# Quantised feed-forwards that turn shifted floats on TensorE, and a GpSimd sum taken in halves

## The reference, cut to what matters

```python
# block 0: int8.  lhs is layernorm(x), rhs a 128x128 weight
lhs_scale = max(|lhs| over features, 1e-12) / 127
q_lhs = clip(round(lhs / lhs_scale), -127, 127)
out = (q_lhs @ q_rhs) * lhs_scale * rhs_scale
# block 1: ternary weight, 8 bit rows
z = clip(x / a_scale * 127, -128, 127);  y = round(z) @ w_quant.T * (w_scale * a_scale / 127)
# block 3, SwitchHead: 8 heads h, 8 experts e, two of them chosen per row and head
xv  = einsum('bsd,hedp->bshep', x, v_w);   v = einsum('bshep,bshe->bhsp', xv, gate_v)
ctx = softmax(q k / sqrt(P)) @ v
out = einsum('bshep,hepd->bsd', ctx[..., None, :] * gate_o[..., None], o_w)
```

## Time and profile before

| | us |
|---|---|
| median of 3 runs | 3508.23 |
| the profiled execution | 3510.38 |
| its span, from first to last instruction | 3508.5 |
| busy in the span: PE, DVE, ACT, POOL | 3139.7, 3014.5, 2281.8, 2265.1 |
| feed-forward of layer 0 | about 209 to 297 |
| feed-forward of layer 1 | about 641 to 717 |
| SwitchHead stage | about 1575 to 3508 |

### The profile page before, as it was taken

The page is one execution under the profiler, slowest core; times in us unless marked ns, Lnnn a source line. Parts: engine busy times, 40 slices in busy tenths (PEclk is TensorE's granted clock), DMA queues, the critical chain, the costliest instruction groups (busy, mean ns, idle before and its releaser), DMA issues.

```text
span 3508.5 us, 80049 instructions
## 1 busy us (share of the span) xinstructions
PE 3139.7 (89%) x24877; PEld 2286.1 (65%) x24890; DVE 3014.5 (86%) x9644; ACT 2281.8 (65%) x7501; POOL 2265.1 (65%) x2884
## 2 busy tenths in 40 slices
PE   6944999369986599949999999999999999999999
PEld 3522777246654377737777777777777777777777
DVE  4455999679989799958999999999999999999998
ACT  2355666721139666646777777777777777777777
POOL 1246999444448766615777777777777777777777
PEclk9999999555557699969999999999999999999999
DMA  1101000011100001140000000000000000000000
GB/s 53 56 4 19 16 16 14 1 45 45 45 21 1 10 29 31 30 121 6 8 8 8 8 7 8 8 8 7 7 8 8 8 8 8 8 8 8 8 7 6
DMA packets 135142, 63.82 MB, mean 18 GB/s; under 512 B 22592, under 2 KB 134336, under 8 KB 134720
## 3 DMA queue, kind: packets, MB, share of 16 engines
q1 hardware_dynamic: 134720, 58.70, 6.1%
HBM read 41.81 MB, written 8.45 MB: 14 GB/s over the span
## 4 chain that ended last, share of the span: by engine, by line
PE 43%; DVE 10%; issue 1%; POOL 0%; ACT 0%; DMA 0%; POOLq 0%; SPq 0%; DVEq 0%; ACTq 0%
PE ps_sw_d L1968 16%; PE ps_sw_a L1968 15%; DVE sw_o_part L1870 6%; PE ps_sw_w L2010 4%; PE ps_sw_w L1997 3%; PE ps_sw_s L1983 2%; PE ps_sw_s L2021 2%; DVE sw_gate_v L1900 1%; DVE sw_ctx_low L1916 1%; PE ps_sw_m L1988 1%; DVE sw_m_inv L1897 0%; PE ps_sw_m L1976 0%; DVE sw_mv L220 0%; DVE sw_v_part L1870 0%; DVE sw_norm L1898 0%
## 5 line engine op out<-in xcount | busy, mean ns | idle before, releaser
L1756 ACT ACTIVATE sw_scaled<-ps_sw_a,sw_gate_o 128x128 f32<-128x128 f32 x2048 | 620.5, 447 | 251.5 <-PE ps_sw_a L1968 243.4
L1756 ACT ACTIVATE sw_scaled<-ps_sw_a,sw_gate_v 128x128 f32<-128x128 f32 x2048 | 597.3, 445 | 217.3 <-PE ps_sw_a L1968 217.1
L1723 POOL TENSOR_TENSOR sw_o_rest<-sw_o_rest,sw_scaled 128x512 f32<-128x512 f32 x384 | 498.7, 1299 | 200.6 <-ACT sw_scaled L1756 199.2
L1870 DVE SCALAR_TENSOR_TENSOR sw_o_part<-ps_sw_d,sw_gate_o,sw_o_part 128x128 f32<-128x128 f32 x1920 | 555.5, 338 | 26.5 <-PE ps_sw_d L1968 25.3
L1703 POOL TENSOR_TENSOR sw_v_pair<-sw_v_part,sw_scaled 128x256 f32<-128x256 f32 x512 | 377.1, 737 | 248.3 <-DVE sw_v_part L1870 164.8
L1870 DVE SCALAR_TENSOR_TENSOR sw_v_part<-ps_sw_d,sw_gate_v,sw_scaled 128x128 f32<-128x128 f32 x1024 | 302.6, 335 | 90.1 <-PE ps_sw_d L1968 86.7
L1870 DVE SCALAR_TENSOR_TENSOR sw_v_part<-ps_sw_d,sw_gate_v,sw_v_part 128x128 f32<-128x128 f32 x1024 | 302.5, 334 | 0.0
L1708 POOL TENSOR_TENSOR sw_v<-sw_v_pair 128x128 f32<-128x128 f32 x512 | 235.8, 460 | 40.2
L920 POOL TENSOR_TENSOR at_key_wide<-at_keyT,c_half_heads 128x1024 f32<-128x1024 f32 x128 | 242.6, 1896 | 4.2 <-ACT at_keyT L1017 4.2
L1968 PE MATMUL ps_sw_a<-sw_v_high,sw_xT_high 128*128 128x512 f32 x512 | 225.9, 441 | 0.3 <-ACT sw_scaled L1756 0.3
L1968 PE MATMUL ps_sw_a<-sw_o_high,sw_ctx_high 128*128 128x512 f32 x512 | 214.6, 419 | 0.0
(11 more groups left out here) (314 smaller groups left out, 8897.6 us busy)
## 6 DMA issues: line engine op xcount, KB each, us to landing
at_ctxT<-ctx_T SPq DMA_DIRECT2D x128, 64.0 KB, 1.8
re_values<-in_ctx SPq DMA_DIRECT2D x128, 64.0 KB, 2.3
x<-in_x SPq DMA_DIRECT2D x64, 64.0 KB, 1.8
l_ctx<-in_ctx SPq DMA_DIRECT2D x64, 64.0 KB, 2.0
re_ctx<-in_ctx SPq DMA_DIRECT2D x64, 64.0 KB, 1.9
scratch_x<-x SPq DMA_DIRECT2D x64, 64.0 KB, 1.8
swp_staged<-in_L_ffn_v_w SPq DMA_DIRECT2D x8, 512.0 KB, 5.5
swp_staged<-in_L_ffn_o_w SPq DMA_DIRECT2D x8, 512.0 KB, 6.9
```

The costliest lines, as they stand in the source:

```text
L1723: pool.tensor_tensor(o_rest[:], o_rest[:], scaled[:, h % 4], ALU.add).then_inc(pooled["o"], 1)
L1756: act.activation(scaled[:, h % 4, e], ps_a[h % 2][:, e], ACT.Copy, scale=gates[:, s, h, HALF_E + e:HALF_E + e + 1]).then_inc(a_scaled[kind ...
L1870: dve.scalar_tensor_tensor(out=acc[:, e % 2], in0=ps_d[h % 2][:, e], scalar=gates[:, s, h, e:e + 1], in1=before, op0=ALU.mult, op1=ALU.add ...
```

## The change

Three edits.

1. In both quantised feed-forwards DVE's subtraction L716 and its buffer go. PE turns the shifted floats themselves, 32 bits wide, into a PSUM bank of floats. ACT's copy out of that bank adds -ROUND and writes bf16.
2. The lags behind it shrink by one: turning 4 to 3, copy and product 5 to 4, output and POOL's add 6 to 5. The shift's buffer is free when it has been turned, no longer when it has been rounded.
3. In the SwitchHead stage each of POOL's sums into `o_rest` becomes two of 128x256, the second behind a wait for the first.

```diff
-        q16 = k.sb(name + "_q16", [P, NB, N, P], BF16)
-        ps_q = [k.psum(f"{name}_q{n}", [P, N, P], BF16) for n in range(2)]
+        ps_q = [k.psum(f"{name}_q{n}", [P, N, P]) for n in range(2)]
...
-                in_order(([(0, spread)] if layer == 0 else []) + [(6, add), (1, rstd)], GROUPS)
+                in_order(([(0, spread)] if layer == 0 else []) + [(5, add), (1, rstd)], GROUPS)
...
-                def rounded(g, s):
-                    dve.wait_ge(q["shifted"], N * g + N)
-                    if g >= NB:
-                        dve.wait_ge(q["turned"], g - NB + 1)
-                    dve.tensor_scalar(q16[:, s], shifted[:, s], ROUND, None, ALU.subtract).then_inc(q["rounded"], 1)
...
-                steps += ([(3, output_scale)] if layer == 1 else []) + [(4, rounded), (1, variance)]
+                steps += ([(3, output_scale)] if layer == 1 else []) + [(1, variance)]
...
-                    act.activation(qT[:, s], ps_q[g % 2], ACT.Copy).then_inc(q["qT"], 1)
+                    act.activation(qT[:, s], ps_q[g % 2], ACT.Copy, bias=-ROUND).then_inc(q["qT"], 1)
...
-                        act.wait_ge(q["rounded"], g - NB + 1)
+                        act.wait_ge(q["turned"], g - NB + 1)
...
-                in_order([(6, output), (2, normalise), (5, keep), (3, shift)], GROUPS)
+                in_order([(5, output), (2, normalise), (4, keep), (3, shift)], GROUPS)
...
-                    pe.wait_ge(q["rounded"], g + 1)
+                    pe.wait_ge(q["shifted"], N * g + N)
...
-                        m = pe.transpose(ps_q[g % 2][:, n], q16[:, s, n], C["ident16"][:])
+                        m = pe.transpose(ps_q[g % 2][:, n], shifted[:, s, n], C["ident"][:])
...
-                in_order(([(0, turn_rows)] if layer == 0 else []) + [(5, product), (4, turned)], GROUPS)
+                in_order(([(0, turn_rows)] if layer == 0 else []) + [(4, product), (3, turned)], GROUPS)
...
-                            pool.tensor_tensor(o_rest[:], scaled[:, 0], scaled[:, 1], ALU.add).then_inc(pooled["o"], 2)
+                            pool.tensor_tensor(o_rest[:, 0:2], scaled[:, 0, 0:2], scaled[:, 1, 0:2], ALU.add)\
+                                .then_inc(q["o_half"], 2)
+                            pool.wait_ge(q["o_half"], u + 1)
+                            pool.tensor_tensor(o_rest[:, 2:4], scaled[:, 0, 2:4], scaled[:, 1, 2:4], ALU.add)\
+                                .then_inc(pooled["o"], 2)
...
-                            pool.tensor_tensor(o_rest[:], o_rest[:], scaled[:, h % 4], ALU.add).then_inc(pooled["o"], 1)
+                            pool.tensor_tensor(o_rest[:, 0:2], o_rest[:, 0:2], scaled[:, h % 4, 0:2], ALU.add)\
+                                .then_inc(q["o_half"], 1)
+                            pool.wait_ge(q["o_half"], u + 1)
+                            pool.tensor_tensor(o_rest[:, 2:4], o_rest[:, 2:4], scaled[:, h % 4, 2:4], ALU.add)\
+                                .then_inc(pooled["o"], 1)
```

More of the change, by code:

```diff
@@ L632, in feed_forward_int @@
         ps_rows = [k.psum(f"{name}_rows{n}", [P, N, P]) for n in range(2)] if layer == 0 else None
-        ps_q = [k.psum(f"{name}_q{n}", [P, N, P], BF16) for n in range(2)]
+        ps_q = [k.psum(f"{name}_q{n}", [P, N, P]) for n in range(2)]
         ps_y = [k.psum(f"{name}_y{n}", [P, N, P]) for n in range(2)]
         q = k.sems(name, "spread", "rows", "added", "stats", "moments", "var_eps", "rstd", "nmr", "xhat", "absmax", "scale",
-                   "inverse", "out_scale", "shifted", "rounded", "turned", "qT", "product", "y", "weighed", "x")
+                   "inverse", "out_scale", "shifted", "turned", "qT", "product", "y", "weighed", "x")
         y_scale = small["scale"] if layer == 0 else small["out_scale"]
@@ L1650, in switch_attention @@
                    "ranked", "u", "uT", "scores", "top", "shift", "exp", "p_turned", "p_kept", "rsum",
-                   "ctx", "ctx_high", "ctx_low", "v", "v_paired", "o_first", "o_added", "o_paired", "y")
+                   "ctx", "ctx_high", "ctx_low", "v", "v_paired", "o_first", "o_added", "o_paired", "o_half", "y")
         a_made = {n: k.sem("sw_a_made_" + n) for n in "vo"}
```

## The result

| | before | after |
|---|---|---|
| median of 22 runs each | 3507.18 | 3493.86 |
| the profiled execution's span | 3508.5 | 3495.5 |

What follows compares the result with a forecast made beforehand. It took a DVE-POOL loop to bound layer 0, ACT layer 1, PE with DVE waits the SwitchHead stage. -7.5 - 1.2 + 2.8 - 11.4 = -17.3 us, from 3508.2 to 3491; forecast's own range 3486 to 3499, whole range 3475 to 3515.

Steps and rivals of the forecast that it cites:

- part 1: Layer 0's feed-forward: removing L716 and shortening the lag saves 7.5 us, between 3 and 9.
- So POOL becomes the bound, at 4.28: Layer 0's feed-forward: without L716 the slot falls from 4.72 to POOL's 4.28 us, 0.44 saved in some 11 slots.
- The two terms ahead of the drain: Layer 0's feed-forward: -4.8 us from some 11 steady slots and -0.5 from earlier slots without large POOL work.
- The drain, -2.5: End of layer 0's feed-forward: the shorter lag leaves POOL three pairs instead of four, saving 2.5 us.
- part 3: SwitchHead stage: halving POOL's sums saves 11.4 us in the steady tiles and costs 2.8 at the end.
- Part 2: Layer 1's feed-forward: ACT stays full, so only start and drain gain; -1.2 us, between +1 and -2.5.
- Both DVE waits of PE go or nearly so: SwitchHead stage: L1900 ends 0.35 us earlier, so PE's bank d loads hardly wait for DVE's sums.
- ACT's hold on the a load: SwitchHead stage: ACT's sums for o unit 7 become what PE's bank a load waits for, allowing it at 2057.80.
- the 0.19: SwitchHead stage: us saved per tile once ACT is the next bound; over some 60 tiles -11.4 us.
- 12 x 0.23: End of the SwitchHead stage: 12 unhidden POOL sums, each 0.23 us longer when halved, cost 2.8 us.
- Rival (c): SwitchHead stage: L1900 meets the second half of POOL's sum and ends 0.4 us later; 3520 us, chance 0.19.
- Rival (d): Layer 1's feed-forward and retention: denser turns raise PE's clock from 0.50 to 1.00; 3477 us, chance 0.04.

Runs made afterwards that it cites:

- e17: Changed kernel with the feed-forwards' absolute maxima and moments in PSUM and whole POOL sums in the last tile; 0.9950 of the kernel before, 17.7 us less.
- e6: Changed kernel with the old, longer lags in the feed-forwards; layer 0 86.5 us against the changed kernel's 84.6, layer 1 75.5 against 74.4.
- e3: Changed kernel with whole instead of halved POOL sums in the last SwitchHead tile; 0.9960 of the kernel before, 14.0 us less.
- e8: Changed kernel with unread extra PE matmuls in layer 1's feed-forward to keep PE busy; 0.9958 of the kernel before.

## Why the prediction was wrong

Two steps failed: one in the sum of part 1, worth 4 us, and one that the sum doesn't have at all, worth 20.

**The step that failed in part 1 is "So POOL becomes the bound, at 4.28".** DVE's removed 0.49 us did leave the loop of DVE and POOL, but the slot fell by 0.17, not 0.44. I compared three bounds and left out a fourth, the loop of the rows above, which was 4.55 us long all the time. I missed it because I took DVE's durations as fixed. The scale was 0.47 long, of which 0.15 is its own; the rest was waiting for POOL's L651. Whenever the scale starts, it ends with POOL's multiplication, 1.29 us after that began before the change and 1.30 after it: it started 0.82 us behind and took 0.47, now it starts 0.66 behind and takes 0.64. The two terms ahead of the drain were forecast at -4.8 and -0.5 and are -1.5 together. e17 took the lock away and kept the order, and the slot was 4.25: the 4.28 was POOL's right bound, the lock the missing term. The low end of the range, "the three near-equal bounds trip over each other at 4.5", had the size, without the mechanism. The drain, -2.5, measured -1.95 (e6 1.85).

**The total against the measured ratio.** -17.3 us was forecast, 0.9951 or 3491. The ratio of 0.9905 makes it 3475, far below the forecast's own range of 3486 to 3499. The step that failed here is that the sum holds the three touched stages only and puts all others at nothing: the first stage took 47 us less in e17, and seven of 21 executions against two of 22 were in that group. Group against group it is 0.9964 or 3495.6, inside the range, and the 4.7 us that lack there are part 1's 4 and half a us of part 3. The rows of before could have warned that the clock of the first stage had room: the same 32-bit turn takes 0.42 us there and 0.27 in the second attention, while the clock column reads 1.00 in both.

```profile
L337 PE MATMUL ps_l_turn<-c_ident,l_ctx x64: 417/421/422, 33.6 to 182.7; 128*128 128x128 f32 x64
...
L1064 PE MATMUL ps_at_turned<-c_ident,at_probs x1024: 272/273/406, 333.9 to 1519.3; 128*128 128x128 f32 x171
```

**Part 2** held: -1.25 against -1.2, slot 4.18. Its care for a slower turn at clock 0.50 had no object: four turns take 1.11 us in layer 1 as in layer 0.

**Part 3** held in size: tile 29.73 as forecast, first to last normalisation 11.6 us shorter against 11.4, the drain +3.5 against +2.8. L1901 at 372 ns (forecast 350). Its way was only half right. "Both DVE waits of PE go or nearly so" failed: three of 0.23 us remain. ACT's hold on the a load came where it was said, 0.24 us. All these waits together are 0.94 us a tile, no less than the 0.89 before, so the 0.19 can't be read off them, and that it came out to the hundredth is in part luck. The drain costs more than 12 x 0.23: a load of PE for bank a waits 1.00 us for ACT at 3481.84, where none waited before. In e3 such a load waits 0.67 us, and there ACT itself waits 1.3 us for POOL; for the changed kernel the trace doesn't name POOL. Rival (c), the second half, didn't come: L1901 at 2046.52 starts 0.28 us before the first half ends at 2046.80, and its longest instance is 556 ns.

**Rival (d)** didn't come: the clock stayed at 0.50 in layer 1's feed-forward and the retention, and e8's busier PE didn't change the retention's. It had the right resource, the clock, in the wrong stage.

## What to carry to other kernels

A DVE instruction's duration in a trace may be mostly waiting for POOL; compare it with its shortest instance before you take it as a constant, and draw every loop that passes through it, also those that are a little shorter than the one that binds now. Small statistics that sit on a loop between DVE and POOL can lie in PSUM; that took 0.3 us a slot off here, where reordering had only moved the wait about. Plot the single times before you trust a ratio: two groups drawn unevenly made 13 us look like 33.

## What the runs showed of the hardware

- A stream of 32-bit turns and small products with PE never idle (20.00 of 20 us) ran 150 us at the lower clock level in 19 of 20 profiles and at the higher from 39 us on in one (e17); 0.42 against 0.27 us for the same turn.
- In the first 325 us the granted-clock column reads 1.00 also where the durations are those of the lower level (turn of 0.48 us at 321.8, 0.33 at 325.6, after the change). Read the clock there from durations.
- scalar_tensor_tensor with two SBUF inputs waits for POOL as tensor_scalar does; the same work read from PSUM doesn't (0.64 against 0.15 us).
- A small VectorE instruction that meets a GpSimd multiplication ends with it, however early it began: the scale took 0.47, 0.64 and 1.23 us in three orders and ended each time within 0.03 us of GpSimd's multiplication.
